# Max passes of a graph network on one core: nine one-step buffers in the room of three nine-gather buffers, each folded and stored by itself

## The reference, cut to what matters

```
def _pool_max(h, edge_src, edge_dst):
    pooled = segment_max(h[edge_src], edge_dst, num_segments=N)
    cnt = segment_sum(ones, edge_dst, num_segments=N)
    return where(cnt > 0, pooled, 0)

h1 = relu(embeddings @ Wp1.T + bp1);            p1 = _pool_max(h1, src, dst)
x = relu(concat([embeddings, p1]) @ Wm1.T + bm1); p2 = _pool_max(x, src, dst)
x = layernorm(relu(concat([x, p2]) @ Wm2.T + bm2) + x)
p3 = _pool_max(x, src, dst)
x = layernorm(relu(concat([x, p3]) @ Wm3.T + bm3) + x)
```

## Time and profile before

| what | value |
| --- | --- |
| three runs, median (lowest to highest) | 5532.19 us (5524.11 to 5537.15) |
| the profiled execution: span from the first to the last instruction (no device time of its own is given) | 5536.0 us |
| POOL busy | 3489.2 us (63%), 3686 instructions |
| DVE busy | 3357.0 us (61%), 6781 instructions |
| ACT busy | 1170.9 us (21%) |
| PE busy | 1120.6 us (20%) |
| gathers of the three passes (L533) | 2349, busy 2233.6 us, 951 ns each, POOL idle before them 1135.8 us |
| folds (L559) | 2349, 476 to 477 ns each |
| state copies L597, L599 | 783 each, 601 and 383 ns |
| DMA | 1039.51 MB, 188 GB/s over the span |

### The profile page before, as it was taken

How to read it: one execution, slowest core, us unless ns; L and a number is a source line. 1 busy time by engine, 2 the same in 40 slices (tenths; PEclk the granted TensorE clock), 3 DMA queues, 4 the chain that set the end, 5 groups by cost and what they waited for, 6 DMA issues and landing times. The chain is left out here.

```text
span 5536.0 us, 24899 instructions
## 1 busy us (share of the span) xinstructions
PE 1120.6 (20%) x4017; PEld 728.3 (13%) x4017; DVE 3357.0 (61%) x6781; ACT 1170.9 (21%) x2663; POOL 3489.2 (63%) x3686
## 2 busy tenths in 40 slices
PE   5333321105222221006222200019400000000005
PEld 4222211004111110005111100016200000000003
DVE  7676666554434434336355433338479888898896
ACT  4222222222222222224222222225100000000001
POOL 4566666665666666665676666654466666666653
PEclk7555555557555555557555555559755555555557
DMA  5555555554555655556555655554477677776763
GB/s 178 170 170 172 173 169 187 183 188 136 197 184 192 203 183 195 185 189 187 199 190 197 217 179 188 188 171 153 139 224 215 212 216 216 224 220 208 218 186 109
DMA packets 325739, 1039.51 MB, mean 188 GB/s; under 512 B 71351, under 2 KB 124740, under 8 KB 292172
## 3 DMA queue, kind: packets, MB, share of 16 engines
q0 software_dynamic: 209408, 628.59, 38.1%
q1 hardware_dynamic: 116172, 409.34, 19.9%
HBM read 649.96 MB, written 388.11 MB: 188 GB/s over the span
## 5 line engine op out<-in xcount | busy, mean ns | idle before, releaser
L533 POOL DMA_INDIRECT G<-tab,ix x2349 | 2233.6, 951 | 1135.8 <-issue 699.7
L559 DVE SCALAR_TENSOR_TENSOR G<-tail,pass_lists,G 128x256 f32<-128x256 f32 x1566 | 696.4, 477 | 1217.8 <-DMA G<-tab,ix 526.8
L1869 POOL DMA_INDIRECT kv<-kvtab,dst_ix x936 | 889.1, 950 | 428.1 <-issue 283.1
L597 ACT ACTIVATE tail<-G 128x512 f32<-128x512 f32 x783 | 470.6, 601 | 1600.4 <-issue 607.7
L599 ACT ACTIVATE wide<-G 128x256 f32<-128x256 f32 x783 | 300.1, 383 | 949.8 <-DVE G L559 521.4
L674 PE MATMUL tail<-weights,hT 128*128 128x256 f32 x588 | 305.0, 674 | 766.3 <-issue 499.6
L559 DVE SCALAR_TENSOR_TENSOR G<-wide,pass_lists,G 128x256 f32<-128x256 f32 x783 | 372.6, 476 | 111.7 <-issue 84.4
L2058 PE MATMUL trio<-ident,state 128*128 128x128 f32 x6 | 2.0, 430 | 1476.8 <-DVEq L2080 1476.8
L674 PEld LDWEIGHTS tail<-weights,hT 128*128 128x128 f32 x588 | 172.7, 324 | 848.9 <-issue 529.1
L1918 DVE TENSOR_TENSOR kv<-kv,wide 128x3072 f32<-128x3072 f32 x78 | 260.8, 3343 | 29.0 <-DMA kv<-kvtab,dst_ix 28.9
L1934 DVE TENSOR_REDUCE s<-kv 128x96 f32<-128x3072 f32 x78 | 260.8, 3343 | 0.0
(11 more groups left out here) (361 smaller groups left out, 3602.7 us busy)
## 6 DMA issues: line engine op xcount, KB each, us to landing
hist<-G SPq DMA_DIRECT2D x261, 1152.0 KB
G<-tab,ix POOLq DMA_INDIRECT x2349
ahist<-state SPq DMA_DIRECT2D x78, 408.0 KB
tab<-o SPq DMA_DIRECT2D x147, 128.0 KB
kv<-kvtab,dst_ix POOLq DMA_INDIRECT x936
h<-tab SPq DMA_DIRECT2D x98, 128.0 KB
G<-tab SPq DMA_DIRECT2D x98, 128.0 KB
kvtab<-U SPq DMA_DIRECT2D x49, 256.0 KB
```

What stands on the lines that cost most here:

```text
L533: g.indirect_dma_start(G[b][:, k, :], None, tab, bass.IndirectOffsetOnAxis(ix[:, b, k:k + 1], 0)).then_inc(s_eg[b].sem, 16)
L559: ins = v.scalar_tensor_tensor(out=G[b][:, k, :], in0=state2 if c == 2 else state[:, c, :], scalar=reset[:, at:at + 1], in1=G[b][:, k, :], ...
L597: a.activation(state, of[:, 0:2, :], ACT.Copy).then_inc(c_state.sem, 1)
L1869: g.indirect_dma_start(kvs[n % KB][:, k, :], None, kvtab, bass.IndirectOffsetOnAxis(dst_ix[:, at:at + 1], 0)).then_inc(s_kv[n % KB], 16)
```

## The change

The three buffers stay where they are, but each third of one (three gathers, one step) gets its own pair of semaphores, nine slots in all (`RING = UB * STEPS`): `s_in[r]` counts the slot's gathers in, `s_kept[r]` its store.

- POOL still waits once a batch for the indices, and now before the first gather of each step for the store of the same slot three batches earlier (not at all in the first three batches).
- DVE waits for the gathers three times a batch, before the first fold of each step, for three gathers each.
- SP stores each step by itself when its third fold is done: three DMAs of 384 KB (3072 bytes a partition) in place of one of 1152 KB.
- Folds, copies, fillers, `place` after the sixth fold and their order on each engine stay as they are.

```
+        RING = UB * STEPS
+        s_in = [Count(sem(f"s_in{r}")) for r in range(RING)]
+        s_kept = [Count(sem(f"s_kept{r}")) for r in range(RING)]
...
                     def gather(i, b):
                         g.wait_ge(c_eix.sem, c_eix.of(i, b, UB))
-                        g.wait_ge(s_hs[b].sem, s_hs[b].base + i * 16)
                         for k in range(J):
-                            g.indirect_dma_start(...).then_inc(s_eg[b].sem, 16)
+                            r = b * STEPS + k // C
+                            if k % C == 0 and i:
+                                g.wait_ge(s_kept[r].sem, s_kept[r].base + i * 16)
+                            g.indirect_dma_start(...).then_inc(s_in[r].sem, 16)
...
-                            if k == 0:
-                                v.wait_ge(s_eg[b].sem, s_eg[b].base + (i * (16 * J) + 16 * J))
+                            if c == 0:
+                                arrived = s_in[b * STEPS + j]
+                                v.wait_ge(arrived.sem, arrived.base + (i + 1) * (16 * C))
...
                     def store(i, b):
-                        sp.wait_ge(c_fold.sem, c_fold.base + 2 + 2 * STEPS * (i * UB + b + 1))
-                        sp.dma_start(hist_p[:, bass.ds((i * UB + b) * J, J), :], G[b][:, :, :]).then_inc(s_hs[b].sem, 16)
+                        for j in range(STEPS):
+                            step = (i * UB + b) * STEPS + j
+                            sp.wait_ge(c_fold.sem, c_fold.base + 2 * (step + 2))
+                            sp.dma_start(hist_p[:, step * C:(step + 1) * C, :], G[b][:, j * C:(j + 1) * C, :]).then_inc(s_kept[b * STEPS + j].sem, 16)
```

More of the change, by code:

```diff
@@ L202, in gnn_kernel @@
         s_tile = [Count(sem(f"s_tile{b}")) for b in range(UB)]
-        s_eg = [Count(sem(f"s_eg{b}")) for b in range(UB)]
+        RING = UB * STEPS
+        s_in = [Count(sem(f"s_in{r}")) for r in range(RING)]
+        s_kept = [Count(sem(f"s_kept{r}")) for r in range(RING)]
         s_hs = [Count(sem(f"s_hs{b}")) for b in range(UB)]
@@ L530, in gather @@
                         g.wait_ge(c_eix.sem, c_eix.of(i, b, UB))
-                        g.wait_ge(s_hs[b].sem, s_hs[b].base + i * 16)
                         for k in range(J):
-                            g.indirect_dma_start(G[b][:, k, :], None, tab, bass.IndirectOffsetOnAxis(ix[:, b, k:k + 1], 0)).then_inc(s_eg[b].sem, 16)
+                            r = b * STEPS + k // C
+                            if k % C == 0 and i:
+                                g.wait_ge(s_kept[r].sem, s_kept[r].base + i * 16)
+                            g.indirect_dma_start(G[b][:, k, :], None, tab, bass.IndirectOffsetOnAxis(ix[:, b, k:k + 1], 0)).then_inc(s_in[r].sem, 16)
                     staged(g, NB, UB, [(0, gather), (0, side.pool(g))])
@@ L579, in store @@
                     def store(i, b):
-                        sp.wait_ge(c_fold.sem, c_fold.base + 2 + 2 * STEPS * (i * UB + b + 1))
-                        sp.dma_start(hist_p[:, bass.ds((i * UB + b) * J, J), :], G[b][:, :, :]).then_inc(s_hs[b].sem, 16)
+                        for j in range(STEPS):
+                            step = (i * UB + b) * STEPS + j
+                            sp.wait_ge(c_fold.sem, c_fold.base + 2 * (step + 2))
+                            sp.dma_start(hist_p[:, step * C:(step + 1) * C, :], G[b][:, j * C:(j + 1) * C, :]).then_inc(s_kept[b * STEPS + j].sem, 16)
                     staged(sp, NB, UB, tiles.sync(sp) + [(0, store)] + (ahead.sync(sp) if ahead else []))
                     side.last_sync(sp)
-                    for b in range(UB):
-                        sp.wait_ge(s_hs[b].sem, s_hs[b].base + (NB // UB) * 16)
+                    for kept in s_kept:
+                        sp.wait_ge(kept.sem, kept.base + (NB // UB) * 16)
                 @blk.tensor
@@ L614, in max_pass @@
             c_state.close(2 * NB * STEPS)
-            for b in range(UB):
-                s_eg[b].close(NB // UB * 16 * J)
-                s_hs[b].close(NB // UB * 16)
+            for r in range(RING):
+                s_in[r].close(NB // UB * 16 * C)
+                s_kept[r].close(NB // UB * 16)
             if marks:
```

## The result

The changed kernel takes 5506.78 us (median of 13 runs, 5494.21 to 5534.34), the kernel before 5532.19 us (13 runs of its own, 5519.37 to 5544.53). The ratio is 0.9964, with a 95% interval of 0.9952 to 0.9976: 25 us faster, where 200 were forecast and the range ended at 5480. The profiled execution has a span of 5510.8 us.

A forecast was written before the change was run, and what follows sets the result against it. The prediction took POOL's queue of gathers plus 414 us of pauses as the bound. Its terms, -60 - 60 - 65 - 15 = -200 us against the profiled 5536.0, gave 5336, so 5332 us as median, range 5195 to 5480.

The forecast's parts named there:

- The bound: Three passes: POOL's gathers at 1.25 us each plus 414 us of pauses, waiting for a buffer or its indices.
- Pass 1, -60: Pass 1: folds starting after three gathers save two thirds of DVE's 95.5 us of waits for gathers, -60 us.
- Pass 2, -60: Pass 2: small stores release buffers sooner and remove half of 120 us of POOL's pauses, -60 us.
- pass 3, -65: Pass 3: -36 us from its last 37 batches and -30 from the other 50, taken as -65 us.
- Late in pass 3, -36: Last 37 batches of pass 3: from 476 to 440 us, 11.9 us each, between POOL's 11.28 and the chain's 12.6.
- Drains, -15: End of each pass: last folds finish 3.3 to 6 us sooner after the last gather, -15 us for three passes.
- The added waits at 0: POOL's two more waits a batch lie within the 0.30 us before every gather, DVE's are hidden: cost 0.
- The small stores at the same rate: DMA engines: each third of a store holds them 0.94 us at the large store's rate, nothing added.
- The stretched stops: Rival: DVE's long stops end because gathers have drained, so they lengthen with POOL's lead; -85 us, 5447 us, chance 0.25.
- The sign that the prediction named for it: Waits before L637 and L825 longer than 168.3 us and 14 us each while POOL's lead grows.
- no change: Rival: new waits are met as late as the old, `place` and late folds set every pause; within 11 us, chance 0.04.
- the slower ones: Rivals: late hand-overs at each step, +136 us, chance 0.05; small stores keeping DMA engines from gathers, +104 us, chance 0.02.

The follow-up runs named there:

- e13: Changed kernel with `place` after the third fold in passes 1 and 3 and a small memset behind each gather in pass 2: 5567.24 us, before 5536.85.
- e14: Changed kernel with a 128x256 memset behind each gather in passes 1 and 2, eight gathers of nine in pass 3 (wrong result): 5410.74 us, before 5543.47.
- e7: Kernel before with only the change's waits for gathers per step, stores left whole: 5529.39 us, ratio 0.9988 to the kernel before.
- e8: Kernel before with only the change's three small stores, all nine gathers awaited before the first fold: 5542.93 us, ratio 1.0009 to the kernel before.
- e15: Changed kernel with a 128x216 memset behind each gather of pass 1 alone: 5516.3 us, ratio 0.9964 to the kernel before.
- e9: Kernel before with TensorE's product of every third tile computed nine times over, for stops of known length: 5815.58 us.
- e10: Changed kernel with TensorE's product of every third tile computed nine times over: 5790.75 us.
- e5: The changed kernel itself, run again on a chip of the fast kind: 4913.13 us, ratio 0.9967 to the kernel before.
- e2: Kernel before with `place` after the third fold instead of the sixth, fast kind of chip: 4921.2 us, ratio 0.9996 to the kernel before.
- e3: Changed kernel without stores during the passes (wrong result), fast kind of chip: 980.8, 979.2 and 984.3 us of gathering in the passes.

## Why the prediction was wrong, point by point

*The bound.* "The kernel is bound by POOL's queue of gathers plus pauses" took 0.95 + 0.30 = 1.25 us for the cost of a gather and all 414 us above it for something that waits could regain. That is the step that failed. On this kind of chip no pass of any run gathered faster on average than 1.40 us (1.401 and 1.397 in passes 2 and 3 before, 1.406 and 1.402 after, 1.404 in e13, 1.407 in e14 with fewer gathers; up to 1.42 in e7, e8 and e15), and the pauses are how the rest is paid. By that, 1167.6 - 1096 = 71 us were to be gained in pass 1, and nothing in passes 2 and 3. That the pauses can't be regained is shown by e13, e14 and the changed kernel itself; what sets the 1.40 us stays open. The number stood in the rows: 1111 and 1104 us for passes with quite different fillers, stores that ended pauses in the one and none in the other.

*Pass 1, -60.* The term came true where it was read (95.5 to 11.9 us of waits for gathers) and false in what it is worth: 16 us. The stops before L637 were taken as fixed ("its 168.3 us before L637 stay"). They stay in sum and change in kind, and e9 and e10 show that a stop for the same work grows by 2 to 3 us when VectorE comes to it earlier, since it ends when it ended before.

*Pass 2, -60, and pass 3, -65.* That "remote" was a store ("as I read it") is wrong: 72 of the 115 us in pass 2 and 107 of 109 in pass 3 were the late count of `place`. The earlier trace rows was a pause of the rarer sort. Even so `place` isn't the cause, as e13 shows; a pause ends with whichever count is waited for. Both passes gained nothing (+3.7, +3.8).

*Late in pass 3, -36.* The last 37 batches were to shrink from 476 to 440 us. By POOL's gathers they went from 467 to 472, and the 50 before them from 627 to 626 where -30 was forecast. The chain at 4.20 us a step, three steps 12.6 us, was read rightly; that the batch could be shortened to 11.9 was not. 12.6 us is nine times 1.40, and it is no limit of folds and copies: on the fast kind (e5) the same 37 batches take 417 us, 11.3 each.

*Drains, -15.* The term was the time from last gather to last fold, 3.3 to 6 us less a pass. Here that gave 4 us in all and nothing in pass 1 (9.3 and 9.4), and some 8 more came from behind the last folds, which the term didn't contain: that the two together come near 15 is luck. On the fast kind the drains proper gave 9 us (6.6, 6.5 and 6.7 to 3.8, 3.8 and 3.1) and the smaller last store 5.

*The added waits at 0* held: on a fast chip 0.30 us stands before every gather, waiting or not. *The small stores at the same rate* held too. One reading there was wrong, without weight in the sum: gathers do land inside a store of 1152 KB, 95 of 783 in e2's pass 1, though the stores take 30% of it. DMA issues of e5 and then of e2 (KB each, us from issue to landing):

```profile
hist<-G SPq DMA_DIRECT2D x783, 384.0 KB, 2.8
```

```profile
hist<-G SPq DMA_DIRECT2D x261, 1152.0 KB, 4.9
```

The Trainium skill ("DMA: Bandwidth & Descriptors", Anatomy of one DMA) gives, for a DMA that GpSimd issues, 2.0 us and the bytes at 436 GB/s, an estimate of 2.9 and 4.7 us, and the trace agrees, though SyncE issues these. Going against the rule of 1 MiB a transfer in the Trainium skill ("DMA: Bandwidth & Descriptors", Bandwidth), weighed in the prediction, costs nothing here, where the DMA engines are used to 0.68 at most.

*The rivals.* The stretched stops had 0.25 and the right mechanism, with a price of 85 us that was too high, since it still left pass 3 and the short pauses to be regained. The sign that the prediction named for it, longer stops in sum, did not show in the changed kernel (189 and 185 us at `keep` in pass 1); only e9 and e10 bring it out. The true time lies between that rival and no change. Neither of the slower ones came.

## What to carry to other kernels

When several stretches with different work come out at the same time per item, here 1.40 us a gather, that time is likely the bound, and the waits inside are only how it shows; divide before adding up pauses, and test it. A wait that "nothing in the trace" ends is to be looked up in the semaphore's own times before it is given a cause. A stop may end at a time of its own, whenever the engine comes to it, so a reckoning with stops of fixed length counts a gain that the machine takes back. And a program that looks bound on one chip should be run on a second before it is rebuilt around what the first shows.

## What the runs showed of the hardware that was not expected

- Two kinds of chip. The kernel before takes 4923 to 4932 us on three chips and 5532 to 5543 us on the others. The instructions last the same (a gather 0.950 us in e5's pass 1, 0.948 in the changed kernel's), and so do a gather's packets on the DMA engines (median 0.159 us and mean 0.23 us in both traces). The granted clock of the kernel is 0.55 to 0.56 on both.
- On the slow kind, while gathers are issued every 1.25 us, counts of VectorE, TensorE and POOL come late: within 0.03 us in the good case, over 5 us for VectorE's folds and 20 us for TensorE's product at worst. VectorE's late ones lie on a grid of 0.70 us, half of 1.40. Between the passes, where nothing is gathered, late ones go on for up to 12 us behind the last gather, and then none is late. These traces also caught fewer changes of VectorE's counts: 1556 in the passes of the changed kernel, 2788 in e5, the same kernel. Whether taking the trace has a part in the lateness isn't shown; the traced execution took 5512.59 us, within the range of the others.
- A long stop of VectorE for TensorE's product ended 4.7 to 4.9 us after POOL's last gather in 31 of 34 stops of pass 1 in e9 and e10, whenever the product was done.
- The lateness vanishes at 1.446 us a gather (e14), has shrunk at 1.337 (e13: no late count of VectorE, POOL's own awaited late in 45 places, TensorE's up to 5.8 us late) and is partly there at 1.412 in pass 1 (e15), so it isn't a matter of the pace alone.
- What takes 1.40 us a gather is open. It isn't the stores' number (three a batch or one, the same), nor the DMA engines' share (0.52 to 0.63 there, 0.62 to 0.68 on the fast kind). e3, the test without stores, met only the fast kind, and smaller gathers were not tried.
